# Attention 1 in turns of three half tiles, seven pooled additions into two buffers, and the queries' operand two steps later

## What is computed

```
q = proj(layernorm(x), Wq);  k, v = proj(ctx, Wk), proj(ctx, Wv)
scores = clip(q @ k.T / sqrt(32), -50, 50)
scores = clip(where(mask, scores, -10000), -50, 50)
probs  = softmax(scores)                      # over 1601 context rows
probs  = probs / (probs.sum() + 1e-8)
ctx    = probs @ v
```

## Time and profile before

| | |
|---|---|
| median of 3 runs | 2752.97 us (2752.05 to 2756.59) |
| the profiled execution, device time | 2758.67 us |
| its span, first to last instruction | 2756.8 us |
| busy, share of the span | PE 94%, DVE 67%, ACT 45%, POOL 44% |
| mean granted TensorE clock | 0.981 |
| DMA moved | 400.61 MB, mean 145 GB/s |

### The profile page before, as it was taken

One profiled execution on the slowest core, in us unless ns is written; L12 is line 12 of the kernel. 1 busy time (PEld: TensorE's weight loads), 2 busy tenths in 40 slices (PEclk: granted clock), 3 DMA queues, 4 the chain that ended last, 5 costly groups with the idle time before them and its releaser, 6 DMA issues. The chain is left out here.

```text
span 2756.8 us, 35478 instructions
## 1 busy us (share of the span) xinstructions
PE 2583.9 (94%) x14009; PEld 1671.8 (61%) x14024; DVE 1842.0 (67%) x2545; ACT 1248.4 (45%) x1869; POOL 1204.4 (44%) x298
## 2 busy tenths in 40 slices
PE   8999999998999999999978998997999999997898
PEld 8888888885444444544426777776333434334776
DVE  5554544456676766767764766553899999997664
ACT  3222312214656565665642222222778778883211
POOL 1000000005999999999940000000677777774110
PEclk9999999999999999999999999999999999998899
DMA  8677666564534435344107534436967777762100
GB/s 294 239 232 258 251 228 246 176 192 116 122 68 93 97 65 121 67 97 93 62 4 256 191 134 164 150 118 167 191 150 152 150 153 150 153 186 100 62 31 31
DMA packets 214855, 400.61 MB, mean 145 GB/s; under 512 B 16696, under 2 KB 92504, under 8 KB 214624
## 3 DMA queue, kind: packets, MB, share of 16 engines
q1 hardware_dynamic: 214688, 398.34, 51.9%
HBM read 256.31 MB, written 140.33 MB: 144 GB/s over the span
## 5 line engine op out<-in xcount | busy, mean ns | idle before, releaser
L1300 POOL TENSOR_TENSOR pooled<-pooled,probs 128x2048 f32<-128x2048 f32 x140 | 641.1, 4579 | 22.1 <-ACT probs L1174 2.5
L1174 ACT ACTIVATE probs<-psum 128x512 f32<-128x512 f32 (+1 forms) x832 | 459.3, 598 | 373.4 <-PE psum L1071 370.4
L1201 DVE TENSOR_REDUCE win_max<-psum 128x1 f32<-128x802 f32 x480 | 453.7, 987 | 169.8 <-PE psum L1036 169.6
L2009 DVE TENSOR_SCALAR probs<-psum,bound 128x1024 f32<-128x1024 f32 (+1 forms) x416 | 507.4, 1277 | 44.5 <-PE psum L1905 44.5
L1964 ACT ACTIVATE probs<-probs 128x1024 f32<-128x1024 f32 (+1 forms) x416 | 440.6, 1059 | 113.3 <-DVE probs L2009 75.4
L2040 POOL TENSOR_TENSOR pooled<-pooled,probs 128x2048 f32<-128x2048 f32 x80 | 368.3, 4604 | 80.5 <-ACT probs L1964 80.5
L1071 PE MATMUL psum<-q_st,k_st 128*128 128x512 f32 (+1 forms) x832 | 336.8, 439 | 36.1 <-ACT den_sb L1186 17.9
L1071 PEld LDWEIGHTS psum<-q_st,k_st 128*128 128x128 f32 (+1 forms) x832 | 149.4, 186 | 258.5 <-ACT probs L1174 175.7
L215 POOL TENSOR_TENSOR r_q<-ve_q,minus_half 128x4 f32<-128x4 f32 x8 | 8.7, 1086 | 669.8 <-DVE ve_q L191 669.8
L1036 PE MATMUL psum<-k_st,q_st 96*128 96x402 f32 x960 | 266.6, 359 | 6.4 <-DVE o_sb L1232 5.2
L1905 PE MATMUL psum<-q_st,k_st 128*128 128x512 f32 (+1 forms) x832 | 250.8, 423 | 11.0 <-PEq L156 10.5
(11 more groups left out here) (252 smaller groups left out, 4373.6 us busy)
## 6 DMA issues: line engine op xcount, KB each, us to landing
k_st<-k_hi SPq DMA_DIRECT2D x64, 801.0 KB, 11.8
k_st<-k_lo SPq DMA_DIRECT2D x48, 801.0 KB, 11.4
k_hi<-kt_hi SPq DMA_DIRECT2D x32, 801.0 KB, 4.0
k_lo<-kt_lo SPq DMA_DIRECT2D x32, 801.0 KB, 5.8
v_rows<-v_out SPq DMA_DIRECT2D x96, 256.0 KB
v_st<-v_rows SPq DMA_DIRECT2D x24, 768.0 KB
q_st<-q_hi SPq DMA_DIRECT2D x64, 256.0 KB, 11.0
w<-w_hi_d SPq DMA_DIRECT2D x64, 256.0 KB, 3.1
```

Of the source, the lines that this page charges most:

```text
L1174: A.activation(probs[i % NPROBS][0:rows, j, :], bank(score_banks.where["score", u, t, j])[0:rows, :], ACT.Exp, scale=1.0 / ROOT).then_inc( ...
L1201: V.tensor_reduce(win_max[:, r, j, c:c + 1], window(windows.where["max", u, i])[:, :, 0:MV], AX.XY, ALU.max).then_inc(max_done, 1)
L1300: G.tensor_tensor(pooled[u % 2][:], before[:], probs[tile(u, k) % NPROBS][:], ALU.add).then_inc(pool_added, 1)
L2009: V.tensor_scalar(probs[i % NPROBS][0:rows, half * W:half * W + W, :], window(("score", u, t, half))[0:rows], bound[0:rows, u // NG, t:t + 1],
```

## The change

In the first feed-forward stage the transposes of the queries' rows, their splits and the 12 pieces and products behind them come two pieces later (one step f): 8 empty pieces in place of 6 on PE and ACT, 3 in place of 1 on DVE.

In attention 1 a unit is walked in 9 turns in place of 13 steps: a turn scores three half tiles (the ninth two), then takes values and sums of one or two tiles, by a list. Tiles 11 and 12 are taken in turns 0 and 1 of the next unit. The pooled tiles are 8 (0, 1, 3, 4, 6, 7, 9, 10; the last unit leaves out the 10), so 7 additions on POOL and 5 sums on PE besides the pooled one; the pooled sums alternate between two buffers, and POOL's first addition of unit u waits for the sum of unit u-2. `acc` is copied by ACT in turn 1 as soon as its last values are in, `den` in turn 2; `compact` and the inversion come at the end of turn 4, `scaled` and the output at the end of turn 6.

```diff
                     def queries(b):
-                        for _ in range(6):
+                        for _ in range(8):
                             yield
...
                         yield from norm_on_dve(own, nq, rows[b % 2], xn, b, xn_done)
-                        yield
+                        for _ in range(3):
+                            yield
...
-            POOLED = [0, 1, 3, 5, 7, 9, 11]
-            FIRST_SUM, LAG, W, NPROBS, CLOSE = 2, 2, 2, 6, 8
+            POOLED = [0, 1, 3, 4, 6, 7, 9, 10]
+            FIRST_SUM, W, NPROBS = 2, 2, 6
             HALVES = HPG // W
+            PER_TURN, COMPACT, SCALED, ACC_COPY, DEN_COPY = 3, 4, 6, (1, 0), (2, 0)
+            VALUES = [[-2], [-1], [0, 1], [2], [3, 4], [5], [6, 7], [8], [9, 10]]
+            TURNS = len(VALUES)
...
-                pooled = sbuf(f"pooled{n}", [P, HPG, S])
+                pooled = [sbuf(f"pooled{n}{i}", [P, HPG, S]) for i in range(2)]
...
+                def pooled_tiles(u):
+                    return POOLED if u < UNITS - 1 else POOLED[:-1]
...
+                def turns():
+                    for u in range(UNITS + 1):
+                        for k in range(TURNS if u < UNITS else 2):
+                            halves = range(PER_TURN * k, min(PER_TURN * (k + 1), TT * HALVES)) if u < UNITS else ()
+                            values = [divmod(u * TT + v, TT) for v in VALUES[k] if u * TT + v >= 0]
+                            yield u, k, [(u, *divmod(h, HALVES)) for h in halves], values
...
+                        elif t == TT - 1:
+                            m.then_inc(accumulated, 1)
...
+                    for u, k, halves, behind in turns():
+                        for half in halves:
+                            scores(*half)
+                        for tile_behind in behind:
+                            values(*tile_behind)
+                            sums(*tile_behind)
+                        if u and k == COMPACT:
+                            compact(u - 1)
+                        if u and k == SCALED:
+                            scale(u - 1)
+                    compact(UNITS - 1)
+                    scale(UNITS - 1)
...
+                    for u, k, halves, _ in turns():
+                        for i, half in enumerate(halves):
+                            exps(*half)
+                            if u and (k, i) == ACC_COPY:
+                                copy_acc(u - 1)
+                            if u and (k, i) == DEN_COPY:
+                                copy_den(u - 1)
+                    copy_acc(UNITS - 1)
+                    copy_den(UNITS - 1)
...
+                    for u, k, halves, _ in turns():
+                        for half in halves:
+                            clip(*half)
+                        if u and k == COMPACT:
+                            invert(u - 1)
+                        if u and k == SCALED:
+                            output(u - 1)
...
                             if k == 1:
-                                if u:
-                                    G.wait_ge(summed, u)
+                                if u >= 2:
+                                    G.wait_ge(summed, u - 1)
                                 before = probs[tile(u, POOLED[0]) % NPROBS]
                             else:
                                 G.wait_ge(pool_added, adds(u) + k - 1)
-                                before = pooled
-                            G.tensor_tensor(pooled[:], before[:], this[:], ALU.add).then_inc(pool_added, 1)
+                                before = pooled[u % 2]
+                            G.tensor_tensor(pooled[u % 2][:], before[:], this[:], ALU.add).then_inc(pool_added, 1)
```

More of the change, by code:

```diff
@@ L1855, in v_count @@
                     return 32 * (u // 2 + 1) - (0 if u % 2 else 32)
+                def pooled_tiles(u):
+                    return POOLED if u < UNITS - 1 else POOLED[:-1]
                 def adds(u):
-                    return u * (len(POOLED) - 1)
+                    return sum(len(pooled_tiles(v)) - 1 for v in range(u))
                 def pool_reads(u, t):
[L1862 to L1868, removed]
+                    return adds(u) + max(pooled_tiles(u).index(t), 1)
+                def turns():
[4 more added lines that the diff above has]
+                            yield u, k, [(u, *divmod(h, HALVES)) for h in halves], values
                 def pe_program():
@@ L1875, in take, with compact @@
                         return psum[:, 2 * slot:2 * slot + 2, :]
-                    def closing(u):
-                        for _ in range(CLOSE):
-                            yield
+                    def compact(u):
                         ps = take(("compact", u))
@@ L1886, in closing, with scale @@
                         windows.freed_by(inverted, u + 1)
-                        for _ in range(CLOSE):
-                            yield
+                    def scale(u):
                         ps = take(("scaled", u))
@@ L1919, in values @@
                                          pr[0:rows, j, :], start=(t == 0), stop=(t == TT - 1))
-                        if t in POOLED:
+                        if t in pooled_tiles(u):
                             m.then_inc(tile_read, 1)
+                        elif t == TT - 1:
+                            m.then_inc(accumulated, 1)
                     def sums(u, t):
-                        if t not in POOLED:
+                        if t not in pooled_tiles(u):
                             rows, pr = TROWS[t], probs[tile(u, t) % NPROBS]
@@ L1936, in sums @@
                             for j in range(HPG):
-                                m = M.matmul(den[j * DH:(j + 1) * DH, :], ones[:], pooled[:, j, :],
+                                m = M.matmul(den[j * DH:(j + 1) * DH, :], ones[:], pooled[u % 2][:, j, :],
                                              start=False, stop=True)
                             m.then_inc(summed, 1)
[L1941 to L1957, removed]
+                    for u, k, halves, behind in turns():
[10 more added lines that the diff above has]
+                    scale(UNITS - 1)
                 def act_program():
@@ L1964, in exps, with copy_acc @@
                         A.activation(dst, dst, ACT.Exp, scale=1.0 / ROOT).then_inc(exp_done, 1)
-                    def copy_out(u):
-                        A.wait_ge(summed, u + 1)
+                    def copy_acc(u):
+                        A.wait_ge(accumulated, u + 1)
                         if u:
@@ L1970, in copy_out, with copy_den, invert @@
                         A.activation(acc_sb[:], acc, ACT.Copy).then_inc(acc_copied, 1)
+                    def copy_den(u):
+                        A.wait_ge(summed, u + 1)
                         A.activation(den_sb[:], den, ACT.Copy).then_inc(den_copied, 1)
[L1973 to L1978, removed]
+                    for u, k, halves, _ in turns():
[7 more added lines that the diff above has]
+                    copy_den(UNITS - 1)
                 def dve_program():
-                    def closing(u):
-                        for _ in range(CLOSE):
-                            yield
+                    def invert(u):
                         den_cols = window(("compact", u))[:, 0, 0:RT * HPG]
@@ L1992, in closing, with output @@
                                                op0=ALU.add, op1=ALU.mult).then_inc(inverted, 1)
-                        for _ in range(CLOSE):
-                            yield
+                    def output(u):
                         if u:
@@ L2005, in clip @@
                             pu, pt = divmod(i - NPROBS, TT)
-                            if pt in POOLED:
+                            if pt in pooled_tiles(pu):
                                 V.wait_ge(pool_added, pool_reads(pu, pt))
@@ L2013, in dve_program @@
                     V.memset(ones[:], 1.0).then_inc(set_up, 1)
[L2014 to L2025, removed]
+                    for u, k, halves, _ in turns():
[5 more added lines that the diff above has]
+                            output(u - 1)
+                    invert(UNITS - 1)
+                    output(UNITS - 1)
                 def pool_program():
                     for u in range(UNITS):
-                        for k in range(1, len(POOLED)):
-                            t = POOLED[k]
+                        for k in range(1, len(pooled_tiles(u))):
+                            t = pooled_tiles(u)[k]
                             this = probs[tile(u, t) % NPROBS]
```

2 lines of the change are left out of this document (1 added, 1 removed).

## The result

The changed kernel took 2762.96 us in the median of 7 runs (2758.10 to 2767.72) against 2754.11 for the kernel before on the same chips: ratio 1.0031, 95% interval 1.0018 to 1.0044. A second measurement later gave 1.0022 (1.0013 to 1.0032). It is slower by 0.2 to 0.3%, where 1.0% faster was forecast and 2712 to 2739 us was the range.

A forecast was written before the change was run, and what follows sets the result against it. POOL's additions were taken to bound attention 1 at 34.2 us a unit. Savings of 22.9 there (with `acc`'s copy) and 5.4 at the queries, 28.3 together, took 2752.97 to 2725 us, range 2712 to 2739.

The forecast's parts named there:

- the inversion holds the next clip back by 0.63: Attention 1, DVE: the inversion delays the clip behind it by 0.63 us, the output by about as much.
- the sum for DVE: DVE's time per unit of attention 1: 26 clips of 1.20 us plus 1.3 for inversion and output, 32.5 us.
- The third rival: Attention 1: POOL's additions lengthen beside DVE and ACT; at 5.03 us each the total is 2764, slower; chance 0.05.
- PE's switches: Attention 1, PE: going between scores and values or sums costs 0.33 us; 13 switches a unit become 9, saving 1.32.
- the chain of POOL: Attention 1: tile 3's exp, then additions 4.75 us apart without a gap, then the pooled sum: 34.2 us a unit.
- the chain's first link: Attention 1: the exp of tile 3's second half ends 4.75 us after turn 2 starts; POOL adds from 4.8.
- PE, DVE and windows: Attention 1: PE's 33.1 us a unit plus four waits of 0.16 for a clip's window, 33.7 us.
- The whole stretch: Attention 1 from first scores to last pooled sum: 41.4 + 478.8 + 30.4 = 550.6 us against 573.0.
- The queries' part: Feed-forward stage: later transposes of the queries' rows shorten two stalls of PE, saving 5.4 us (2 to 10).
- rival 1: Attention 1: POOL is not the bound; 33.7 us a unit, total 2718, or 33.1 and 2710; chance 0.20.
- rival 2: Attention 1: PE's switches don't shrink, their 0.33 us being waits for clips and exps; total 2738; chance 0.15.
- rival 4: Attention 1: late third half, pooled sum and windows give back all that is saved; total 2753; chance 0.04.

The follow-up runs named there:

- experiment 1: The changed kernel with the inversion's middle result `unity` in PSUM instead of SBUF: 2729.37 us, ratio 0.9904 to the kernel before.
- experiment 9: experiment 1 with tile 10 summed by PE and not by POOL, six additions in place of seven: 2733.82 us, ratio 0.9929.
- experiment 4: The kernel before with its closing one step later (`CLOSE` 12 in place of 8), so the inversion falls into an addition of POOL: 2784.34 us, ratio 1.0103.
- experiment 11: experiment 1 plus a needless 128x16 DVE operation with both operands in SBUF before the output of turn 6: 2807.91 us, ratio 1.0198.

## Why the prediction was wrong

**The step that failed** is the term "the inversion holds the next clip back by 0.63" in the sum for DVE. It was read where the inversion stands between two additions of POOL, and carried over to a place where POOL has no gap, though the same prediction said that six additions follow there "without a gap". It measured 2.4 (3.61 from clip to clip less 1.19), of which 1.65 is the last operation's wait for POOL. That adds 1.33 to a unit: 35.49 in units with the full clock, against 34.16 with the one operand in PSUM. The clock of attention 1, which the prediction took as full and gave no term, adds 1.3 to 1.5 in each unit where it falls. 15 x 1.33 and 10 x 1.4 are 34 us; the stretch from the first scores to the last sum is 586.3 with and 552.2 without.

**The third rival** had the right two engines and the wrong victim. It let POOL's additions grow; they stay at 4.60, and DVE waits for them. I had set the Trainium skill's sentence on shared ports against the length of the additions alone. The Trainium skill, GPSIMD Engine Reference, Specifications, says more exactly that the contention is with VectorE's instructions in a two-port mode or with two SBUF inputs. The traces agree with the second half (0.17 us against 1.83, 2.39 and 3.88), and show besides that it is all or nothing: the operation waits for the whole rest of the addition. Which operations run in a two-port mode no row says; but one with a single tensor in SBUF waits too, as the rows below show.

**It stood in the trace of before.** At the end of attention 0 a product of 128x4, `r_first` by itself, lasts as long as an addition of POOL that starts beside it; DVE and POOL, by timeline:

```profile
1429.50 4.52 DVE L195 TENSOR_TENSOR t_first<-r_first 128x4 f32<-128x4 f32 x1 [1.13 <-POOL r_first L215]
...
1429.44 4.56 POOL L1300 TENSOR_TENSOR pooled<-pooled,probs 128x2048 f32<-128x2048 f32 x1
```

The other instances of that line take 0.15 to 0.17. It isn't the only one. Additions of two tensors of 128x512 in SBUF (L1256, L1258), and a scaling with a single tensor in SBUF and a column of factors (L227), stand beside additions of POOL too; DVE, then POOL, by timeline:

```profile
1379.43 4.65 DVE L227 TENSOR_SCALAR f_cols<-f_cols,o_recip 128x512 f32<-128x512 f32 x1
...
1405.35 4.92 DVE L1258 TENSOR_TENSOR f_rows<-f_rows,o_y 128x512 f32<-128x512 f32 x1
...
1416.62 0.69 DVE L1256 TENSOR_TENSOR o_y<-o_y,o_bp 128x512 f32<-128x512 f32 x1
...
1416.72 5.03 POOL L1300 TENSOR_TENSOR pooled<-pooled,probs 128x2048 f32<-128x2048 f32 x1 [2.07 <-ACT probs L1174]
```

L1256 and L1258 take 0.69 where POOL rests and 4.25 to 4.95 in four instances beside an addition; L227 takes 0.47 to 0.49 elsewhere. They end 0.55 (L227: 0.28) behind the addition and not with it, a little less than their own work takes elsewhere. The last two rows show the other direction: here the operation of DVE had started 0.09 earlier, it kept its 0.69, and the addition took 5.03 where the median is 4.58. That is the addition on which rival 3 was built. Of the 252 additions of this trace only two take over 4.65, this one and one of 4.79 at 1409.86, and both started while an operation of DVE with two operands in SBUF was at its own work: here POOL waits for DVE. An operation whose maximum is some thirty times its median was worth a question.

**What held.** With that one wait gone, the rest of the sum can be checked by experiment 1. PE's switches and the chain of POOL: 34.2 us a unit forecast, 34.16 measured, PE released by POOL in all 15 units; taking the chain's first link 0.3 earlier took 0.24 off. PE, DVE and windows: 33.7 forecast; with one block of 0.86 more that would be 34.6, and experiment 9 measured 34.68, with POOL out of the way. The whole stretch: 550.6 forecast, 552.2 measured. The Trainium skill's sentence on the loading of weights (TensorE: Matmul & The Clock Gate, Part 2), taken alone, would leave a switch at nothing and a unit at 35.7 - 0.86 = 34.8 at least, an estimate; the measured 34.16 stands with rows 3. The second buffer: said to be worth nothing, is worth 0.25 a unit. The queries' part: 5.4 forecast, 5.3 measured in the mean of the traces; the stalls of 3.4 and 2.8 are as read from the end of L1675. Total: 28.3 us less forecast, 26.5 measured in experiment 1.

Rivals 1, 2 and 4 fell: rival 1 by 34.16 and 16.4 us of waits for POOL, rival 2 by the length of a unit in experiment 1, rival 4 since what was saved was lost at one instruction. What stays open is why the clock falls behind the same wait of 1.38 us in two units of three. The strict turn in three executions speaks against chance. Waits of 1.0 us (experiment 4) were followed by a fall in 2 units of 15, those of 1.4 in 10, those of 3.5 (experiment 11) in 14; no experiment was made to tell what decides.

## What to carry to other kernels

When an engine's gaps are closed, look for what used the gaps: an instruction of another engine that was short because it fell into one. Beside long additions on GpSimd, let an operation of VectorE read one of its operands from PSUM, or put it where GpSimd rests; that only one tensor lies in SBUF is not always enough, as the scaling of 4.65 us shows; a small operation on the way to a window or to TensorE is the worst place. And read the maximum of a group as well as its mean: what is thirty times the median in one place shows a rule.

## What the runs showed of the hardware

- An operation of VectorE with two tensor operands in SBUF that starts during an addition of GpSimd (128x2048, 4.6 us) waits for the rest of the addition, whatever its own size. 128x4 took 4.52 and ended 0.02 us behind the addition; 128x16 took 1.83, 2.38 and 3.88 and ended 0.03 to 0.04 behind; 128x512 took 4.25 to 4.95 and ended 0.55 behind. With one operand in PSUM 128x16 takes 0.17 and 128x512 0.69 in the same place.
- The waiting goes both ways: of 252 additions of GpSimd in the kernel before only two took over 4.65 (4.79 and 5.03, the median is 4.6), and both had started while such an operation of VectorE was at work.
- One tensor in SBUF can be enough: a scaling of 128x512 (L227) took 4.65 beside an addition and 0.48 elsewhere. Reductions of 128x32 from SBUF (L1207 to L1213), also in attention 0, took 0.17 to 0.19 beside additions, as elsewhere.
- In attention 1 of the changed kernel, waits of 1.4 us by TensorE were followed by some 3 us at 1.2 GHz in 10 units of 15, in three executions, in strict turn of two units with and one without. Such a wait cost up to twice its own length.
